# First layer batch by batch with rows sent in four groups, and units of 176 slots in place of 192 in the second FFN

## The chip, the cores and the metric

The kernel runs on one core of a Trainium2 chip. The metric is the device time in microseconds (us) of one execution. TensorE (PE in the rows, PEld for its weight loads), VectorE (DVE), ScalarE (ACT), GpSimd (POOL) and SyncE (SP) each work through their own instructions in order and wait for one another by semaphores.

## The reference, cut to what matters

```python
# x [4, 256, 256], ctx [4, 256, 64]; two layers, each mixes tokens and then runs an FFN
sim = einsum(Q, K) / ...; threshold = top_k(sim, 76)[..., -1:]        # per row of 256
A = sigmoid(sim) * (sim >= threshold); A = (A + A.T) * 0.5
x = x + tanh(g0) * ((1 - gamma) * layernorm(x) + gamma * A)           # layer 0, mixing
# layer 0, FFN: token n of a batch goes to expert n % 4 (gate/up 256 x 512, down 256 x 256)
x = x + tanh(g1) * (silu(gate) * up) @ down_proj[e]                   # on layernorm(x)
scores = (ctx Wq + bq)(ctx Wk + bk).T / 8 * layernorm(x)              # layer 1, mixing
x = x + tanh(g2) * softmax(where(mask, -inf, scores))
# layer 1, FFN: 64 experts of width 96, the best 8 per token, weights renormalised
x = x + tanh(g3) * sum_over_8(rw * (silu(h w_gate[e]) * (h w_up[e])) @ w_down[e])
```

The 1024 tokens make 8192 pairs of token and expert. Counted from the reference's own inputs, an expert gets 93 to 169 tokens.

## The kernel before

The tokens are eight tiles of 128 rows, two tiles per batch. The kernel has three stretches.

First stretch, all that leads to the rows of the second FFN. VectorE finds the 76th largest of each row of `sim` in ten rounds of eight (`keep_top`, L982: MAX8 and MATCH_REPLACE8 on `work`), adds the transposed adjacency (`mix_adjacencies`, L1012), takes the statistics of the layer norms (`statistics`, L962; GpSimd's `inverse_deviation`, L435, finishes them), adds the first FFN's result (`add_layer0`, L1023), does the masked scores and the softmax (`masked_scores`, L1030, `add_softmax`, L1045), and picks the experts (`choose_experts`, L1061) and the place of each row (`place_rows`, L1074). The order of its calls is written out at L1117 to L1154: the ten rounds of all four batches first, and the rest two batches at a time. The first FFN runs in two halves of two batches: eight steps of `expert_gate_up0` (L597) and `expert_down0` (L587) with 128 tokens each (`TE`, L48), whose product silu times up is GpSimd's (L443). TensorE, ScalarE and GpSimd follow orders written out by hand at L630 to L695, L873 to L919 and L452 to L492. The eight PSUM banks are handed round in the order of the list of fills (L221 to L277); each fill says whose count frees its bank, and all of ScalarE's share one count.

GpSimd sends the rows: `place_rows` on GpSimd (L469) issues 16 indirect DMAs per batch (L478), each of 128 rows of 320 floats, into `expert_rows` in HBM, which has room for 1024 rows per expert. Before the first of them it waits for `rows_cleared` (L475): SyncE's DMA at L349 has by then filled the first `CAP` rows of each of the 64 experts with empty rows, from `empty_rows`, of which `SLOTS` partitions hold `SUBS` rows each.

```python
sp.dma_start(by_expert[:, 0:CAP * ROW].rearrange("e (p n) -> p e n", p=SLOTS),
             empty_rows[0:SLOTS].rearrange("p (a i) d -> p a (i d)", a=1).to_broadcast([SLOTS, NE, SUBS * ROW])).then_inc(rows_cleared, 16)
```

Second stretch, the second FFN, once all 64 sends have landed (L369): 63 fixed units, one per expert 1 to 63, of `CAP` = 192 slots in two halves of `SLOTS` = 96. For each, SyncE loads the rows (L361, ten units ahead) and the weights (L355, L356, eight ahead), TensorE transposes the rows (L704), multiplies with gate and up (L715) and with down (L724), VectorE copies and multiplies (L1203, L1208), ScalarE takes silu and copies the result (L927, L933), and GpSimd scatters it with two indirect DMAs (L499) of 96 rows. Expert 0, and whatever of an expert lies beyond `CAP`, is done in a loop of counted length (L738); it runs once here.

Third stretch: the picks of each token are loaded and summed with its eight weights on TensorE (L770), and stored.

Of the kernel before, what the change touches and what calls it, by code (L numbers as in the profile page):

```python
# [11 lines left out]
ALU = mybir.AluOpType  # L12
ACT = mybir.ActivationFunctionType

P = 128
# [9 lines left out]
SLOTS = 96  # L25
# [9 lines left out]
def gated_layers_kernel(nc, x, ctx_in, mask_ss, mask_bs, g_xattn, g_ffn, wq0, wk0, gamma_raw, gate_up, down,  # L35
# [12 lines left out]
    TE = HALF // NE0  # L48
# [17 lines left out]
    with ExitStack() as stack:  # L66
# [118 lines left out]
        evac = {who: sem(who + "_evac") for who in ("act", "dve")}  # L185
# [35 lines left out]
        F_CTX, F_PROJ, F_SIM, F_SCORE = {}, {}, {}, {}  # L221
        F_CTX[0] = add_fill("ctx", "act")
# [9 lines left out]
        for b in range(B):  # L232
            F_SCORE[b] = add_fill("score", "act")


        F_ADJT, F_XNT, F_YT, F_XNT2, F_LOGIT = {}, {}, {}, {}, {}
        F_GATE, F_UP, F_DOWN = {}, {}, {}

        def add_gate_up_fills(q):
            F_GATE[q], F_UP[q] = add_fill("gate", "act"), add_fill("up", "act")  # L240

        def add_down_fill(q):
            F_DOWN[q] = add_fill("down", "act")

        for fill, name, who in ((F_ADJT, "adjt", "dve"), (F_XNT, "xnt", "act")):
            for b in (0, 1):
                fill[b] = add_fill(name, who)
        for q in range(NE0):
            if q == NE0 - 1:
                F_ADJT[2] = add_fill("adjt", "dve")  # L250
            add_gate_up_fills(q)
            if q:
                add_down_fill(q - 1)
        add_down_fill(NE0 - 1)
        F_XNT[2] = add_fill("xnt", "act")
        F_ADJT[3] = add_fill("adjt", "dve")
        F_YT[0], F_YT[1] = add_fill("yt", "dve"), add_fill("yt", "dve")
        F_XNT[3] = add_fill("xnt", "act")
        add_gate_up_fills(NE0)
        for q in range(NE0 + 1, 2 * NE0 - 1):  # L260
            add_gate_up_fills(q)
            add_down_fill(q - 1)
        F_XNT2[0], F_XNT2[1] = add_fill("xnt2", "act"), add_fill("xnt2", "act")
        add_gate_up_fills(2 * NE0 - 1)
        F_LOGIT[0], F_LOGIT[1] = add_fill("logit", "act"), add_fill("logit", "act")
        add_down_fill(2 * NE0 - 2)
        add_down_fill(2 * NE0 - 1)
        F_RANK = {}
        F_RANK[0], F_RANK[1] = add_fill("rank", "dve"), add_fill("rank", "dve")
        F_YT[2], F_YT[3] = add_fill("yt", "dve"), add_fill("yt", "dve")  # L270
        F_XNT2[2], F_LOGIT[2] = add_fill("xnt2", "act"), add_fill("logit", "act")
        F_XNT2[3] = add_fill("xnt2", "act")
        F_RANK[2] = add_fill("rank", "dve")
        F_LOGIT[3] = add_fill("logit", "act")
        F_RANK[3] = add_fill("rank", "dve")
# [13 lines left out]
        LAYERNORMS = ((0, None), (1, 0), (1, 1), (1, 2), (1, 3), (2, 0), (2, 1), (3, 0), (3, 1), (2, 2), (2, 3), (3, 2), (3, 3))  # L289
# [11 lines left out]
        def xn_t_view(k, b, permuted):  # L301

            if permuted:
                return xn_t[:, k].rearrange("p (f e b g) -> p f e b g", f=2, e=NE0, b=B // 2)[:, b // 2, :, b % 2, :]
            return xn_t[:, k, b * S:(b + 1) * S]
# [99 lines left out]
        def _(pool):  # L405
# [37 lines left out]
            def up_times_silu(half, experts):  # L443
                for e in experts:
                    q = half * NE0 + e
                    emptied(pool, F_UP[q])
                    if q >= 2:
                        pool.wait_ge(bank_filled, F_DOWN[q - 2] + 1)
                    pool.tensor_tensor(h0_t[:, q % 2].rearrange("p i t -> p (i t)"), silu0[:, q % 2], up0[:, q % 2],  # L449
                                       ALU.mult).then_inc(h0_ready, 1)  # L450
# [7 lines left out]
            inverse_deviation(1, 0)  # L458
            inverse_deviation(1, 1)
            up_times_silu(0, range(NE0))  # L460
            for n, b in ((1, 2), (1, 3), (2, 0), (2, 1)):
                inverse_deviation(n, b)
            up_times_silu(1, (0,))
            inverse_deviation(3, 0)
            up_times_silu(1, (1,))
            inverse_deviation(3, 1)
            up_times_silu(1, (2, 3))
# [14 lines left out]
            place_rows(0, 0, 2)  # L482
            inverse_deviation(2, 2)
            place_rows(0, 2, 4)
            inverse_deviation(2, 3)
            place_rows(0, 4, 10)
            inverse_deviation(3, 2)
            place_rows(0, 10, 13)
            inverse_deviation(3, 3)
            place_rows(0, 13, PICKS)  # L490
            for b in range(1, B):
                place_rows(b, 0, PICKS)  # L492
# [21 lines left out]
        def _(pe):  # L514
# [49 lines left out]
            for b in range(B):  # L564
                query_times_key(1, F_SCORE, b)

# [20 lines left out]
            def expert_down0(q):  # L587
                i = F_DOWN[q]
                begin(i)
                pe.wait_ge(h0_ready, q + 1)  # L590
                for hc in range(KC):
                    for ic in range(IC):
                        last = pe.matmul(bank(i)[:, hc * TE:(hc + 1) * TE], down_w[:, q % NE0, ic, hc * P:(hc + 1) * P],
                                         h0_t[:, q % 2, ic, :], start=ic == 0, stop=ic == IC - 1)
                last.then_inc(bank_filled, 1)
# [681 lines left out]
```

## Time and profile before

| | |
|---|---|
| median of 3 runs | 417.0 us (415.72 to 417.07) |
| the profiled execution | 417.87 us, of which its span is 416.1 us |
| first stretch, up to the last send's issue | 0 to 201.8 us |
| second stretch, first to last fixed scatter | 214.9 to 371.1 us |
| third stretch, first to last product | 383.0 to 413.5 us |
| busy: PE, DVE, ACT, POOL | 275.1, 210.7, 118.0, 214.0 us |

The times of stretches are read from the start and the duration of the instructions at their ends. A busy engine is not the bound by itself: what ended last is told by the chain of waits and by who stood idle.

### The profile page before, as it was taken

Reading aid. Unit: us, or ns where it says so; the run is one execution under the profiler, and the core shown is the slowest. Engines: PE = TensorE matmul, PEld = TensorE weight load, DVE = VectorE, ACT = ScalarE, POOL = GpSimd, SP = SyncE. Lnnn points to the kernel's source line nnn. Section 1 sums busy time; section 2 is a strip of 40 time slices with the busy share of each in tenths; the row PEclk is TensorE's granted clock in tenths of the full one; section 3 lists DMA queues with packets and bytes.
Section 4 is the critical chain, followed back from the end, with each engine's and each line's share of the span. In section 5 each row is a group of like instructions: output and inputs, shape, how many; then the busy total and the mean of one; then the engine's idle time right before and its main releaser. Section 6 shows DMA issues by size and latency. Waiting matters only on the chain.

```text
span 416.1 us, 5526 instructions
## 1 busy us (share of the span) xinstructions
PE 275.1 (66%) x1546; PEld 230.9 (55%) x1546; DVE 210.7 (51%) x921; ACT 118.0 (28%) x265; POOL 214.0 (51%) x256
## 2 busy tenths in 40 slices
PE   5898177137801610000199999999999999951997
PEld 1335067037800500000189999889999889931886
DVE  0799999989386679000033433343433343340352
ACT  2264353316634500000023333333333333320000
POOL 2622112013267777777327777777777777771000
PEclk9999999557975555555589999999999999995899
DMA  4899995360013333333498888888888887226891
GB/s 132 312 352 306 318 310 192 91 190 2 1 63 113 126 126 127 126 127 138 148 243 267 273 270 277 271 264 274 261 273 269 269 270 229 74 73 234 325 305 64
DMA packets 47374, 84.12 MB, mean 202 GB/s; under 512 B 10453, under 2 KB 28249, under 8 KB 46320
## 3 DMA queue, kind: packets, MB, share of 16 engines
q1 hardware_dynamic: 38128, 64.87, 49.9%
q0 software_dynamic: 9216, 18.90, 13.0%
q8 instruction: 13, 0.21, 0.2%
q14 instruction: 17, 0.14, 0.1%
HBM read 48.07 MB, written 39.85 MB: 211 GB/s over the span
## 4 chain that ended last, share of the span: by engine, by line
PE 52%; DVE 18%; POOL 16%; issue 7%; DMA 4%; ACT 2%; SPq 1%; POOLq 1%; ACTq 0%
PE psum L715 20%; POOL expert_rows L478 14%; PE psum L724 13%; PE psum L770 7%; PE psum L704 5%; DVE work L995 5%; DVE top L991 5%; DVE stats L966 2%; PE psum L536 2%; PE psum L530 2%; DMA sim<-token_picks 1%; POOL token_picks L499 1%; PE psum L604 1%; DVE adj L1000 1%; DMA gu_w<-expert_rows 1%
## 5 line engine op out<-in xcount | busy, mean ns | idle before, releaser
L499 POOL DMA_INDIRECT token_picks<-down_w,target x126 | 117.3, 931 | 54.9 <-issue 41.1
L715 PE MATMUL psum<-gu_w,wgu 128*96 128x192 f32 x504 | 93.7, 329 | 0.0
L715 PEld LDWEIGHTS psum<-gu_w,wgu 128*96 128x96 f32 x504 | 78.0, 165 | 0.6 <-DVE gu_w L1203 0.2
L478 POOL DMA_INDIRECT expert_rows<-x_rows,place_at x64 | 62.4, 975 | 23.8 <-issue 23.8
L724 PE MATMUL psum<-proj_t,gu_w 96*96 96x256 f32 x252 | 64.8, 379 | 0.0
L927 ACT ACTIVATE gu_w<-psum 96x192 f32<-96x192 f32 x63 | 20.6, 326 | 130.0 <-PE psum L715 130.0
L1208 DVE TENSOR_TENSOR gu_w<-gu_w,psum 96x192 f32<-96x192 f32 x63 | 22.1, 350 | 67.1 <-ACT gu_w L927 67.1
L704 PE MATMUL psum<-ident,gu_w 96*128 96x96 f32 x108 | 14.1, 256 | 53.1 <-DMA gu_w<-expert_rows 53.1
L933 ACT COPY down_w<-psum 96x512 f32<-96x512 f32 x63 | 36.6, 581 | 33.9 <-PE psum L724 33.9
L724 PEld LDWEIGHTS psum<-proj_t,gu_w 96*96 96x96 f32 x252 | 41.1, 163 | 7.1 <-DVE gu_w L1208 0.4
L704 PEld LDWEIGHTS psum<-ident,gu_w 96*128 96x128 f32 x108 | 12.5, 148 | 57.6 <-DMA gu_w<-expert_rows 54.4
L1203 DVE COPY gu_w<-psum 128x384 f32<-128x384 f32 x63 | 34.4, 547 | 0.0
L439 POOL TENSOR_TENSOR rstd<-var_eps,minus_half 128x2 f32<-128x2 f32 (+1 forms) x13 | 10.4, 797 | 46.6 <-DVE var_eps L972 46.5
L1202 DVE COPY target<-gu_w 96x2 uint32<-96x2 uint32 x27 | 4.5, 165 | 52.6 <-PE psum L704 52.6
L991 DVE MAX8 top<-work 128x8 f32<-128x256 f32 x72 | 26.8, 413 | 0.0
L995 DVE MATCH_REPLACE8 work<-top,work 128x256 f32<-128x256 f32 x64 | 25.7, 409 | 0.0
L604 PE MATMUL psum<-xn_t,gu_w 128*128 128x128 f32 x128 | 19.0, 316 | 1.7 <-ACT xn_t L832 1.7
L604 PEld LDWEIGHTS psum<-xn_t,gu_w 128*128 128x128 f32 x128 | 18.4, 231 | 2.4 <-issue 1.3
L449 POOL TENSOR_TENSOR h_t<-silu,up 128x256 f32<-128x256 f32 x8 | 6.1, 762 | 23.9 <-ACT up L849 23.6
L770 PE MATMUL psum<-sim,xn_t 128*128 128x256 f32 x32 | 9.9, 480 | 11.0 <-DMA sim<-token_picks 11.0
L1241 DVE TENSOR_TENSOR xs<-psum,scores 128x256 f32<-128x256 f32 x8 | 3.4, 424 | 27.3 <-PE psum L770 27.3
L583 PE MATMUL psum<-ident,x_rows 128*128 128x128 f32 x16 | 3.4, 351 | 20.8 <-ACT x_rows L827 19.8
(177 smaller groups left out, 397.1 us busy)
## 6 DMA issues: line engine op xcount, KB each, us to landing
expert_rows<-empty_rows SPq DMA_DIRECT2D x1, 15360.0 KB, 69.3
wgu<-in_L_ffn_w_gate_up SPq DMA_DIRECT2D x65, 192.0 KB, 2.9
gu_w<-expert_rows SPq DMA_DIRECT2D x28, 240.0 KB, 4.2
proj_t<-in_L_ffn_w_down SPq DMA_DIRECT2D x65, 96.0 KB, 4.0
sim<-expert_rows SPq DMA_DIRECT2D x18, 240.0 KB, 4.3
work<-expert_rows SPq DMA_DIRECT2D x18, 240.0 KB, 4.2
gu_w<-in_L_ffn_gate_up_proj SPq DMA_DIRECT2D x4, 512.0 KB, 8.2
sim<-token_picks SPq DMA_DIRECT2D x2, 1024.0 KB, 4.9
```

Source lines behind the costliest of these rows:

```text
L478: pool.indirect_dma_start(rows_dram, bass.IndirectOffsetOnAxis(ap=place_at[:, t, k:k + 1], axis=0), x_rows[:, t, :], None).then_inc(placed ...
L499: pool.indirect_dma_start(picks_dram, bass.IndirectOffsetOnAxis(ap=target[0:SLOTS, e % T_RING, i:i + 1], axis=0), y_slots[0:SLOTS, n, i, : ...
L604: last = pe.matmul(bank(fill)[:, ic * TE:(ic + 1) * TE], gu_w[:, e, k, c:c + P], xn_t[:, k, half * HALF + e * TE:half * HALF + (e + 1) * T ...
L704: last = pe.transpose(psum[:, e % 2, k * CAP + i * SLOTS:k * CAP + (i + 1) * SLOTS], x_slots[n][0:SLOTS, i, k * P:(k + 1) * P], ident[0:SL ...
L715: last = pe.matmul(psum[0:I1, 2 + e % 2, part * CAP:(part + 1) * CAP], wgu[:, n, k, part * I1:(part + 1) * I1], x_slots_t[:, e % 2, k, :], ...
L724: last = pe.matmul(psum[0:SLOTS, 4 + e % 2, i * D:(i + 1) * D], h1_t[:, e % 2, i * SLOTS:(i + 1) * SLOTS], wd[:, n, :], start=True, stop=True)
L770: last = pe.matmul(psum[:, t, 0:D], diag[:, t % 2, k, :], picks[t % K_RING][:, k * D:(k + 1) * D], start=k == 0, stop=k == TOP_K_EXPERTS - 1)
L933: act.copy(y_slots[0:SLOTS, n].rearrange("p i d -> p (i d)"), psum[0:SLOTS, 4 + e % 2, 0:SUBS * D]).then_inc(y_ready, 1)
L991: dve.max(top8[:, t, r], (work if r else sim)[:, t]).then_inc(top8_ready, 1)
L995: dve.match_replace(work[:, t], top8[:, t, r], (work if r else sim)[:, t], REMOVED).then_inc(rest_ready, 1)
L1203: dve.tensor_copy(x_slots_t[:, e % 2].rearrange("p k n -> p (k n)"), psum[:, e % 2, 0:KC * CAP]).then_inc(xt_copied, 1)
L1208: dve.tensor_tensor(h1_t[:, e % 2], silu1[:, e % 2], psum[0:I1, 2 + e % 2, CAP:2 * CAP], ALU.mult).then_inc(h_ready, 1)
```

## The change

`SLOTS` goes from 96 to 88 and so `CAP` from 192 to 176; the constant that divides a count by `CAP` goes from 683 to 745. `TE` goes from 128 to 64: the first FFN runs batch by batch in sixteen steps of 64 tokens. The orders of TensorE, ScalarE, VectorE and GpSimd are written anew, so that batch 0 goes through the whole first stretch while the later batches are still in their rounds; `keep_top` can be run for some of its rounds. Each kind of fill gets a count of its own. For steps 8 to 15 VectorE multiplies silu and up straight from PSUM in place of ScalarE's copy and GpSimd's product. GpSimd's sends are cut by the `inverse_deviation` calls of the later batches.

```diff
-SLOTS = 96
+SLOTS = 88
-    TE = HALF // NE0
+    TE = S // NE0
@@ fills
+        add_fills(("adjt", 0), ("score", 0), ("score", 1), ("xnt", 0), ("score", 2),
+                  ("gu", 0), ("gu", 1), ("gu", 2), ("adjt", 1), ("gu", 3), ("down", 0),
...
@@ gpsimd
             inverse_deviation(1, 0)
+            up_times_silu(0, 1, 2, 3)
             inverse_deviation(1, 1)
+            inverse_deviation(2, 0)
+            up_times_silu(4, 5, 6, 7)
             inverse_deviation(3, 0)
+            inverse_deviation(1, 2)
             place_rows(0, 0, 2)
+            inverse_deviation(2, 1)
+            place_rows(0, 2, 9)
+            inverse_deviation(3, 1)
+            place_rows(0, 9, PICKS)
+            place_rows(1, 0, 3)
+            inverse_deviation(1, 3)
+            place_rows(1, 3, 5)
             inverse_deviation(2, 2)
+            place_rows(1, 5, 10)
+            inverse_deviation(3, 2)
+            place_rows(1, 10, PICKS)
+            place_rows(2, 0, 3)
             inverse_deviation(2, 3)
+            place_rows(2, 3, 9)
             inverse_deviation(3, 3)
+            place_rows(2, 9, PICKS)
+            place_rows(3, 0, PICKS)
@@ tensor, one step of the first FFN
-            for part, fill in enumerate((F_GATE[q], F_UP[q])):
-                begin(fill)
+            begin(F_GU[q])
+            for part in range(2):
                     for ic in range(IC):
                         for k in range(KC):
-                            last = pe.matmul(bank(fill)[:, ic * TE:(ic + 1) * TE], gu_w[:, e, k, c:c + P],
+                            last = pe.matmul(bank(F_GU[q])[:, at:at + TE], gu_w[:, e, k, c:c + P],
@@ tensor, order (batch 0 and the end)
+            transpose_normed(F_XNT, xn, xn_ready, 0)
...
+            expert_gate_up0(0)
+            expert_gate_up0(1)
+            expert_down0(0)
...
+            expert_down0(15)
+            transpose_y0(3)
+            transpose_normed(F_XNT2, x_rows, x_rows_ready, 3)
             router_logits(3)
             rank_rows(3)
@@ vector, steps 8 to 15
+            def up_times_silu(*which):
+                for q in which:
+                    dve.wait_ge(silu0_ready, q - 2 * NE0 + 1)
+                    dve.wait_ge(down_step, q - 1)
+                    dve.tensor_tensor(h0_t[:, q % 2]..., silu0[:, q % 2], bank(F_GU[q])[:, IC * TE:2 * IC * TE], ALU.mult).then_inc(h0_ready, 1)
@@ vector, order
+            keep_top(1, 0, 2)
+            mix_adjacencies(0)
+            statistics(1, 0)
+            keep_top(1, 2, ROUNDS)
+            keep_top(2, 0, 1)
+            mix_adjacencies(1)
+            statistics(1, 1)
+            keep_top(2, 1, 4)
+            add_layer0(0)
+            statistics(2, 0)
+            keep_top(2, 4, 5)
+            masked_scores(0)
+            keep_top(2, 5, 7)
+            softmax_and_statistics(0)
+            keep_top(2, 7, ROUNDS)
+            choose_experts(0)
+            mix_adjacencies(2)
+            statistics(1, 2)
+            place_rows(0)
+            add_layer0(1)
+            statistics(2, 1)
+            keep_top(3, 0, 1)
+            masked_scores(1)
+            up_times_silu(8)
...
+            place_rows(1)
+            keep_top(3, 7, ROUNDS)
+            add_layer0(2)
+            mix_adjacencies(3)
+            statistics(1, 3)
+            statistics(2, 2)
+            masked_scores(2)
...
+            choose_experts(2)
+            up_times_silu(15)
+            place_rows(2)
+            add_layer0(3)
+            statistics(2, 3)
+            masked_scores(3)
+            softmax_and_statistics(3)
             choose_experts(3)
             place_rows(3)
```

## Rows read from the trace of the kernel before

**Rows 1.** The page: the chain that ended last, by engine, as shares of the span.

```profile
PE 52%; DVE 18%; POOL 16%; issue 7%; DMA 4%; ACT 2%; SPq 1%; POOLq 1%; ACTq 0%
```

**Rows 2.** Timeline of POOL, the sends: start, duration, instruction, idle before it.

```profile
116.09 1.23 POOL L478 DMA_INDIRECT expert_rows<-x_rows,place_at  x1 [5.18 <-issue]
...
131.40 0.73 POOL L439 TENSOR_TENSOR rstd<-var_eps,minus_half 128x2 f32<-128x2 f32 x1
...
132.57 1.04 POOL L478 DMA_INDIRECT expert_rows<-x_rows,place_at  x1 [0.16 <-issue]
...
199.60 0.96 POOL L478 DMA_INDIRECT expert_rows<-x_rows,place_at  x1 [0.30 <-issue]
200.86 0.96 POOL L478 DMA_INDIRECT expert_rows<-x_rows,place_at  x1 [0.30 <-issue]
```

**Rows 3.** DMA issues: size, and us from issue to landing.

```profile
expert_rows<-empty_rows SPq DMA_DIRECT2D x1, 15360.0 KB, 69.3
```

**Rows 4.** Timeline of SP, the issue of that DMA and the next.

```profile
16.19 0.61 SPq L349 DMA_DIRECT2D expert_rows<-empty_rows  x1
40.49 35.63 SPq L355 DMA_DIRECT2D wgu<-in_L_ffn_w_gate_up  x1
```

**Rows 5.** Windows: length; busy PE, PEld, DVE, ACT, POOL; granted clock, DMA share, GB/s.

```profile
50.00:60.00 10.00, 4.95 (x21) 4.24 (x22) 9.86 (x41) 5.02 (x10) 2.16 (x4) 1.00 1.00 333
60.00:66.00 6.00, 6.00 (x53) 6.00 (x52) 6.00 (x26) 2.51 (x7) 1.62 (x3) 1.00 0.70 234
...
72.00:74.00 2.00, 0.47 (x5) 0.28 (x3) 2.00 (x9) 1.48 (x3) 0.26 (x2) 1.00 0.18 49
...
116.00:130.00 14.00, 0.00 (x0) 0.00 (x0) 12.46 (x55) 4.45 (x14) 10.99 (x13) 0.60 0.26 94
```

**Rows 6.** Timeline of DVE: where its blocks begin.

```profile
32.81 0.75 DVE L991 MAX8 top<-sim 128x8 f32<-128x256 f32 x2
...
47.35 0.68 DVE L1016 TENSOR_TENSOR adj<-adj,psum 128x512 f32<-128x512 f32 x1
...
50.07 0.68 DVE L1016 TENSOR_TENSOR adj<-adj,psum 128x512 f32<-128x512 f32 x1
```

**Rows 7.** Windows, columns as in Rows 5: two batches' work on DVE after their rounds.

```profile
110.87:117.00 6.13, 3.92 (x40) 3.48 (x38) 5.71 (x34) 3.85 (x10) 0.95 (x2) 1.00 0.00 0
117.00:132.40 15.40, 0.00 (x0) 0.00 (x0) 13.72 (x59) 4.15 (x12) 12.07 (x16) 0.55 0.29 107
```

**Rows 8.** Timeline of PE: passes with 128 and with 64 columns.

```profile
94.06 5.80 PE L604 MATMUL psum<-xn_t,gu_w 128*128 128x128 f32 x32 [0.74 <-ACT xn_t L832]
...
107.75 1.95 PE L604 MATMUL psum<-xn_t,gu_w 128*128 128x128 f32 x16
109.53 1.90 PE L626 MATMUL psum<-router,xn_t 128*128 128x64 f32 x16
```

**Rows 9.** The chain in order of time: start, us, what, second FFN and end.

```profile
253.79 1.30 PE psum L715 x8
255.10 0.86 PE psum L724 x4
255.96 0.33 PE psum L704 x4
...
383.03 30.50 PE psum L770 x128
```

**Rows 10.** Timeline of POOL, the scatters.

```profile
214.94 0.94 POOL L499 DMA_INDIRECT token_picks<-down_w,target  x1 [13.13 <-ACT down_w L933]
...
355.29 0.91 POOL L499 DMA_INDIRECT token_picks<-down_w,target  x1 [0.78 <-issue]
356.50 0.91 POOL L499 DMA_INDIRECT token_picks<-down_w,target  x1 [0.30 <-issue]
...
371.14 2.88 POOL L499 DMA_INDIRECT token_picks<-down_w,target  x1 [0.30 <-issue]
```

**Rows 11.** Windows of the second FFN, columns as in Rows 5.

```profile
240.00:260.00 20.00, 20.00 (x130) 18.12 (x129) 7.79 (x24) 7.26 (x16) 14.66 (x17) 1.00 0.88 274
```

More of the change, by code:

```diff
@@ L231, in gated_layers_kernel @@
                 F_PROJ[w, half] = add_fill("proj", "act")
[L232 to L262, printed above, removed]
@@ L441, in inverse_deviation @@
                 pool.tensor_tensor(shift[:, n, tiles], neg_mean[:, n, tiles], rstd[:, n, tiles], ALU.mult).then_inc(shift_ready, 1)
[L443 to L448, printed above, removed]
+            def up_times_silu(*which):
+                for q in which:
+                    emptied(pool, F_GU[q])
+                    need(pool, down_step, q - 1)
                     pool.tensor_tensor(h0_t[:, q % 2].rearrange("p i t -> p (i t)"), silu0[:, q % 2], up0[:, q % 2],
@@ new lines, in _ @@
+            expert_down0(4)
+            expert_gate_up0(6)
+            expert_down0(5)
+            expert_gate_up0(7)
+            expert_down0(6)
+            expert_down0(7)
+            pe.wait_ge(consts_ready, 9)
+            transpose_normed(F_XNT2, x_rows, x_rows_ready, 0)
+            pe.wait_ge(ld["router"], 16)
+            router_logits(0)
+            transpose_y0(1)
+            transpose_adj(2)
+            rank_rows(0)
+            transpose_normed(F_XNT, xn, xn_ready, 2)
+            emptied(pe, F_XNT[2])
@@ L980, in _, with keep_top @@
                               ALU.mult).then_inc(evac["dve"], 1)
-            def keep_top(b):
+            def keep_top(b, first, end):
                 emptied(dve, F_SIM[b])
                 tiles = range(b * HB, (b + 1) * HB)
-                for r in range(ROUNDS):
+                for r in range(first, end):
                     for t in tiles:
@@ L1125, in _ @@
+            up_times_silu(8)
+            keep_top(3, 1, 2)
+            up_times_silu(9)
+            softmax_and_statistics(1)
+            keep_top(3, 2, 3)
+            up_times_silu(10)
+            keep_top(3, 3, 4)
+            up_times_silu(11)
+            keep_top(3, 4, 6)
+            choose_experts(1)
+            keep_top(3, 6, 7)
+            place_rows(1)
+            keep_top(3, 7, ROUNDS)
+            add_layer0(2)
             mix_adjacencies(3)
             statistics(1, 3)
-            for b in (0, 1):
-                add_layer0(b)
-                statistics(2, b)
@@ L1146, in _ @@
-            for b in (2, 3):
-                add_softmax(b)
-                statistics(3, b)
-            choose_experts(2)
-            router_weights(0)
-            place_rows(2)
+            statistics(2, 2)
+            masked_scores(2)
+            softmax_and_statistics(2)
+            up_times_silu(12, 13)
+            router_weights(0)
+            router_weights(1)
+            up_times_silu(14)
+            choose_experts(2)
+            up_times_silu(15)
+            place_rows(2)
```

324 lines of the change are left out of this document (166 added, 158 removed).

## The prediction, made before the changed kernel was run

> **What bounds the kernel now.** I read the chain of waits first: it is more than half TensorE, and the rest mostly VectorE and GpSimd [rows 1]. Then the timelines in order of time, since the shares mix three stretches. The reader is to see three different bounds.
>
> In the first stretch VectorE works nearly without a gap until 117 us, and from there GpSimd's sends set the end. They begin at 116.1 and the last ends at 201.8 [rows 2]. One costs 1.26 us from start to start (199.60 to 200.86), and each of the four `inverse_deviation` calls among them 1.17 us (131.40 to 132.57). 64 sends are 81 us and the four calls 5: GpSimd never rests, so the only way to end them earlier is to begin them earlier. In the second stretch TensorE is busy all of 20 us in a window of 20 [rows 11], and one unit is 1.30 + 0.86 + 0.33 = 2.49 us [rows 9]. But GpSimd is right behind: late in the stretch, where it is not waiting, its scatters start 1.21 us apart (355.29 to 356.50), 2.43 per unit [rows 10]. The third stretch (product of 30.5 us, rows 9) isn't touched.
>
> **The change, part by part.** All is counted in the profiled execution, 417.9 us; the median of the runs is 0.9 us below it.
>
> *When can the first send go?* VectorE must do, before batch 0 has its places: the start to 32.8, ten rounds each for batches 1 and 2 (14.5 us each with their last step, 32.81 to 47.35), three mixes with statistics (2.7 us each, 47.35 to 50.07) [rows 6], and batch 0's own rest. Rows 7 give that rest: 13.7 us busy for two batches from adding the FFN's result to the last statistics, 6.9 each; 5.7 for two batches from choice to places, 2.9 each. 32.8 + 29.1 + 8.2 + 6.9 + 2.9 = 79.9. To it come VectorE's waits. Most of TensorE's work for batch 0 (transposes, sixteen passes of gate and up, eight of down for each of four experts) lies beside rounds of batches 1 and 2, but the router's transposes and products stand directly ahead of the choice; I count 5 us for these waits, an estimate: eight of the router's passes at 0.12 [rows 8], a transpose, two copies, and two chains of the same kind (adjacency, FFN result) of which rounds cover only a part. So VectorE's side is ready at about 85, not 115.
>
> *What else must be there?* GpSimd waits for the empty rows ahead of its first send. Before, that wait was free: the DMA is issued at 16.19 [rows 4] and lands 69.3 us later [rows 3], at 85.5, with 30 us to spare. Now there is no slack left, and its shape changes with `SLOTS`: 88 partitions instead of 96. In bytes it is 8% less. How 88 partitions are dealt to 16 DMA engines no row of before shows, since all its transfers have 64, 96 or 128 partitions, all multiples of 16. The bounds: dealt evenly, 69.3 x 88/96 = 63.5 us, landing at 79.7. Dealt in equal parts of whole partitions, only 11 engines can share (8 each), each moving 8 partitions where it moved 6: 69.3 x 8/6 = 92.4 us, landing at 108.6. The windows say that engines differ: busy to the full until 60 us, 70% from 60 to 66, 18% (three of 16) from 72 to 74 [rows 5], and the next SP issue stays stuck from 40.5 to 76.1 behind the full queue [rows 4]. So the average engine ends at about 67 and the slowest near 85. Average times 8/6 from about 20 us, when the loads ahead of it are done: 83; slowest: 107. I take equal parts, and between 88 and 108 the middle, 98: the time depends on whether the slow engines are among the eleven, which no row tells.
>
> The Trainium skill ("DMA: Bandwidth & Descriptors", section "Why a DMA increments its semaphore by 16 and not by 1") speaks against this change: a DMA from SyncE runs on the largest number of engines up to 16 that divides the partition counts of both sides, so 96 gives 16 and 88 gives 11. With the slowest engine among the eleven, the sum would be that of the late rival below; with an even deal that of the early one. No row of before can confirm it.
>
> *From the first send to the last.* GpSimd's own floor is 64 sends and six calls, 64 x 1.265 + 6 x 1.17 = 88 us. The calls are now between the sends, and each waits for VectorE, which in turn goes on only once the call is done: a wait in both directions that was not there. Behind a waiting `inverse_deviation` stand the sends of its own engine. After the first send VectorE still has: ten rounds of batch 3 (14.5), three times 6.9 + 2.9, one mix (2.7), four steps of `up_times_silu` ahead of that and four behind (0.35 each, an estimate, 2.8), the weights of two batches (an estimate, 2): 51 us of work, and it needs TensorE's chain for each batch in turn. Walking the two orders against each other, GpSimd waits 1 us for the places of batch 1, 4 for the statistics of batch 3's mix, 3 to 7 for the places of batch 2, and little for those of batch 3. I take 12: 88 + 12 = 100 us, bounds 90 (nearly all covered) and 105. So the last send ends at 98 + 100 = 198, against 201.8: 3.8 us earlier.
>
> *TensorE in the first stretch.* Twice the steps with half the columns, and half the columns don't make a pass shorter: 16 passes with 128 columns took 1.95 us, 16 with 64 columns 1.90 [rows 8]. So the first FFN's 192 passes (128 in L604, 64 in L593) become 384, 192 x 0.12 = 23 us more. It is hidden where TensorE waited for VectorE's rounds; without that cover it costs all 23, and at the low clock 0.18 per pass (5.80 for 32, rows 8). The granted clock is 1.00 until 66 and 0.55 to 0.60 from 116 to 132 [rows 5, 7], so mostly the lower of the two levels (1.2 GHz in place of 2.4), after TensorE had stood idle. I count that as part of the 12 above.
>
> *ScalarE, PSUM, counts.* Four more table loads and one order more; ScalarE is 4.2 us busy in 15.4 [rows 7] and hides them. The separate counts cost nothing.
>
> *The second FFN.* TensorE: L715 moves 176 columns for 192, L704 88 for 96, L724's 256 stay: 1.30 x 11/12 + 0.33 x 11/12 + 0.86 = 2.35, 0.14 less per unit and 8.8 us in 63. But the scatters don't follow: they are 126 as before. A send of 128 rows has a pitch of 1.265 and a scatter of 96 one of 1.215; by that slope, 0.0016 per row, one of 88 has 1.20. So GpSimd is late next, and the stretch of scatters goes from 371.14 - 214.94 = 156.2 [rows 10] to 125 x 1.205 + 1.5 (the trace has three pauses of 0.5 like that before 355.29) = 152.1: 4.1 us less. The bounds: 1.265, if 88 partitions cost as 128 do, is 159.6, 3.4 us more; 8.8 us less, if GpSimd followed TensorE. The row loads: if on 11 engines, each of these carries 8/6 of its part. The share is 0.88 over all [rows 11], rows being 240 KB of some 670 KB per unit (274 GB/s x 2.5 us); 0.88 x (1 + 0.36 x 0.33) = 0.98. Just short of full, and ten units of lead cover a small lack, so I count nothing, and up to 5 us in the slow case. The loop for expert 0 still runs once: no expert has over 169 tokens, so 176 slots hold each.
>
> The sum: 417.9 - 3.8 - 4.1 = 410.0 us.
>
> **The rivals.**
>
> Early: the empty rows are dealt evenly and land by 80 to 85. Then VectorE sets the first send, at 85, and the last ends at 85 + 100 = 185, the scatters as above: 417.9 - 16.8 - 4.1 = 397.0. For it: the bytes get fewer. Against: 5.5 partitions per engine isn't a whole number.
>
> Late, and slower than before: the DMA with the slowest engines among the eleven lands at 108.6. The sends then end at 208.6, 6.8 us later than before, and batch by batch gains nothing, since the wait for VectorE has become a wait for the clearing. With the scatters 417.9 + 6.8 - 4.1 = 420.6, and up to 425 if the row loads on the same engines slow the units. It decides from a landing at 106 on (106 + 100 - 201.8 = 4.2, what the scatters give). For it: the tail of slow engines [rows 5]. Against: only eleven of sixteen are used, and fewer write at once.
>
> The first stretch is bound by TensorE: the 23 us of passes and the low clock lie on the chain of each batch (transpose, gate and up, down, transpose, logits), and the last send comes 7 us later than forecast, at 205: 417. For it: 0.60 of the clock in the thin part; against: idle TensorE in the same windows.
>
> **How the numbers follow.** Forecast case 0.40, early 0.30, TensorE 0.10, late 0.20. The likeliest is 410. The range goes from 394 (most of the early case) to 422. It leaves out 0.1 on either side. A measurement of this kernel can tell about 0.3%, 1.3 us. Faster: forecast and early, 0.70; same: the TensorE case, 0.10; slower: late, 0.20.
>
> **What would show it.** The landing of `expert_rows<-empty_rows`: by 85, near 98, or past 105; GpSimd's first send right behind it or behind `place_at`. The share of DMA while it runs: about 0.69 (11 of 16) if eleven engines. The last send 98 to 100 us after the first, with 12 us of GpSimd's idle time released by VectorE. In the second FFN TensorE has gaps (2.35 busy of 2.42), and the scatters stand 1.20 apart in every unit. A pitch of 1.26, or units released by DMA, would make the second half wrong; a first send at 85 the first.

## The result and the profile after

The changed kernel takes 456.7 us (median of 4 runs, 455.53 to 459.03) against 416.7 us before (415.72 to 417.07): the ratio is 1.097, with a 95% interval of 1.092 to 1.102. It is 9.7% slower, outside the range of the prediction. The span of the profiled execution is 455.4 us, against 416.1.

The chain that ended last in the changed kernel, as shares of the span (its answer before is [rows 1]):

```profile
PE 34%; POOL 18%; DMA 14%; issue 14%; DVE 9%; another core or an unknown queue 5%; ACT 3%; SPq 1%; POOLq 0%; DVEq 0%; ACTq 0%; PEldq 0%
```

TensorE and VectorE both have less of it; DMA went from 4% to 14% and unexplained waits ("issue") from 7% to 14%. Two of these names mislead. The 5% of "another core or an unknown queue" is the wait for the clearing, 21.6 us from 102.5 on. And of DMA's 14% the page puts 11 on the scatters of the second FFN, whose landing frees the buffers that ScalarE copies into; but GpSimd rests there only its 0.30 us between two scatters, so it is GpSimd that sets the pace, and ScalarE waits behind it. What was lost, and where, is told by the timeline of GpSimd (start, duration, instruction, idle before it and what ended it), which answers to [rows 2, 10]:

```profile
101.47 0.78 POOL L414 TENSOR_TENSOR rstd<-var_eps,minus_half 128x2 f32<-128x2 f32 x1 [12.13 <-DVE var_eps L993]
...
124.41 1.24 POOL L448 DMA_INDIRECT expert_rows<-x_rows,place_at  x1 [21.88 <-DMA expert_rows<-empty_rows]
...
153.83 0.95 POOL L448 DMA_INDIRECT expert_rows<-x_rows,place_at  x1 [7.22 <-issue]
...
161.76 0.72 POOL L414 TENSOR_TENSOR rstd<-var_eps,minus_half 128x2 f32<-128x2 f32 x1 [4.45 <-DVE var_eps L993]
...
190.49 0.96 POOL L448 DMA_INDIRECT expert_rows<-x_rows,place_at  x1 [9.25 <-issue]
...
233.52 0.96 POOL L448 DMA_INDIRECT expert_rows<-x_rows,place_at  x1 [0.31 <-issue]
...
248.87 1.02 POOL L476 DMA_INDIRECT token_picks<-down_w,target  x1 [14.38 <-ACT down_w L954]
...
300.86 0.99 POOL L476 DMA_INDIRECT token_picks<-down_w,target  x1 [0.30 <-issue]
302.16 0.99 POOL L476 DMA_INDIRECT token_picks<-down_w,target  x1 [0.30 <-ACT down_w L954]
...
410.89 1.06 POOL L476 DMA_INDIRECT token_picks<-down_w,target  x1 [0.30 <-issue]
```

The reader is to see four things: the first send comes 8.3 us later than before, not earlier, and GpSimd stood 21.88 us ahead of it until the clearing had landed; it was held up even before that, at 101.5, by VectorE's statistics; there are three long pauses among the sends; and a scatter takes 0.99 us, with 1.30 from start to start. The whole loss can be laid out on these rows:

| piece, us | before | after | difference |
|---|---|---|---|
| start to first send | 116.09 | 124.41 | +8.3 |
| first to last send | 84.77 | 109.11 | +24.3 |
| last send to first scatter | 14.08 | 15.35 | +1.3 |
| first to last fixed scatter | 156.20 | 162.02 | +5.8 |
| from there to the end of the span | 44.96 | 44.51 | -0.5 |
| span | 416.1 | 455.4 | +39.3 |

The windows of the changed kernel, columns as in [rows 5]:

```profile
50.00:60.00 10.00, 10.00 (x50) 10.00 (x49) 2.88 (x9) 0.87 (x4) 0.91 (x2) 1.00 0.68 177
...
78.00:84.00 6.00, 6.00 (x30) 6.00 (x30) 3.43 (x14) 3.93 (x8) 0.63 (x2) 1.00 0.48 102
...
84.00:90.00 6.00, 6.00 (x30) 6.00 (x30) 3.80 (x15) 1.42 (x4) 1.31 (x3) 1.00 0.48 99
...
114.00:120.00 6.00, 0.00 (x0) 0.00 (x0) 0.00 (x0) 0.33 (x1) 0.00 (x0) 1.00 0.58 124
```

In 50 to 60 TensorE is busy throughout and VectorE less than a third, where before VectorE was busy 9.86 of 10 and TensorE half. The DMA share is 0.68, which is 11 of 16, where it was 1.00, and from the early seventies 0.48. From 114 to 120 all four engines stand still but for 0.33 us of ScalarE.

TensorE's timeline has the first FFN's passes, in blocks of 16 and 32, and the router's, answering to [rows 8]:

```profile
43.77 7.09 PE L584 MATMUL psum<-xn_t,gu_w 128*128 128x64 f32 x32
...
58.33 3.52 PE L584 MATMUL psum<-xn_t,gu_w 128*128 128x64 f32 x16
...
94.89 1.94 PE L606 MATMUL psum<-router,xn_t 128*128 128x64 f32 x8 [0.78 <-issue]
```

Sixteen passes of 64 columns take 3.52 us, 0.22 each; in [rows 8] sixteen of them took 1.90, and sixteen of 128 columns 1.95. The router's eight take 0.24 each. The granted clock in these windows is 1.00.

### The profile page after: what moved, and what is told of

The parts are those of the page before. It is cut to its first block, busy times and chain, and to the rows that moved or that the text cites. A ratio compares the mean times of both kernels' runs of the same rounds, so it can differ in the third digit from the quotient of the medians.

```text
span 455.4 us, 5963 instructions
## 1 busy us (share of the span) xinstructions
PE 335.5 (74%) x1738; PEld 282.0 (62%) x1738; DVE 207.3 (46%) x929; ACT 117.7 (26%) x269; POOL 219.1 (48%) x256
## 3 DMA queue, kind: packets, MB, share of 16 engines
q0 software_dynamic: 9216, 18.92, 12.5%
## 4 chain that ended last, share of the span: by engine, by line
PE 34%; POOL 18%; DMA 14%; issue 14%; DVE 9%; another core or an unknown queue 5%; ACT 3%; SPq 1%; POOLq 0%; DVEq 0%; ACTq 0%; PEldq 0%
DMA token_picks<-down_w,target 11%; PE psum L584 9%; POOL token_picks L476 9%; POOL expert_rows L448 7%; PE psum L774 7%; PE psum L570 6%; PE psum L719 3%; DVE top L1011 2%; DVE work L1015 2%; PE psum L728 2%; POOL rstd L414 2%; PE psum L557 1%; PE psum L513 1%; DVE stats L987 1%
## 5 line engine op out<-in xcount | busy, mean ns | idle before, releaser
L719 PE MATMUL psum<-gu_w,wgu 128*96 128x176 f32 x504 | 88.1, 319 | 0.0
L728 PE MATMUL psum<-proj_t,gu_w 96*88 96x256 f32 x252 | 66.3, 385 | 3.7 <-DVE gu_w L1262 3.2
L1262 DVE TENSOR_TENSOR gu_w<-gu_w,psum 96x176 f32<-96x176 f32 x63 | 21.0, 333 | 95.5 <-ACT gu_w L948 90.8
L954 ACT COPY down_w<-psum 88x512 f32<-88x512 f32 x63 | 36.7, 582 | 92.9 <-DMA token_picks<-down_w,target 79.6
L584 PE MATMUL psum<-xn_t,gu_w 128*128 128x64 f32 x256 | 57.1, 421 | 2.2 <-ACT xn_t L831 2.2
L584 PEld LDWEIGHTS psum<-xn_t,gu_w 128*128 128x128 f32 x256 | 55.9, 332 | 4.1 <-ACT xn_t L831 3.4
L728 PEld LDWEIGHTS psum<-proj_t,gu_w 96*88 96x88 f32 x252 | 37.0, 156 | 17.5 <-DVE gu_w L1262 9.5
L570 PE MATMUL psum<-h_t,down_w 128*128 128x64 f32 x128 | 30.1, 422 | 17.4 <-DVE h_t L1056 17.4
L570 PEld LDWEIGHTS psum<-h_t,down_w 128*128 128x128 f32 x128 | 28.8, 332 | 17.6 <-issue 17.6
L1257 DVE COPY gu_w<-psum 128x352 f32<-128x352 f32 x63 | 32.3, 513 | 0.0
L1011 DVE MAX8 top<-work 128x8 f32<-128x256 f32 x72 | 26.8, 413 | 0.6 <-DVE h_t L1056 0.6
```

Source lines behind the costliest of these rows:

```text
L570: last = pe.matmul(bank(i)[:, c:c + TE], down_w[:, e, ic, hc * P:(hc + 1) * P], h0_t[:, q % 2, ic, :], start=ic == 0, stop=ic == IC - 1)
L584: last = pe.matmul(bank(F_GU[q])[:, at:at + TE], gu_w[:, e, k, c:c + P], xn_t[:, k, b * S + e * TE:b * S + (e + 1) * TE], start=k == 0, st ...
L719: last = pe.matmul(psum[0:I1, 2 + e % 2, part * CAP:(part + 1) * CAP], wgu[:, n, k, part * I1:(part + 1) * I1], x_slots_t[:, e % 2, k, :], ...
L728: last = pe.matmul(psum[0:SLOTS, 4 + e % 2, i * D:(i + 1) * D], h1_t[:, e % 2, i * SLOTS:(i + 1) * SLOTS], wd[:, n, :], start=True, stop=True)
L954: act.copy(y_slots[0:SLOTS, n].rearrange("p i d -> p (i d)"), psum[0:SLOTS, 4 + e % 2, 0:SUBS * D]).then_inc(y_ready, 1)
L1011: dve.max(top8[:, t, r], (work if r else sim)[:, t]).then_inc(top8_ready, 1)
```

## The experiments

The theory after the result had three causes. P: with only 64-column passes TensorE is so slow that each batch's chain waits for it. C: the clearing of 88 partitions lands at 124. S: a scatter of 88 rows costs more than one of 96. The rivals: the batch-by-batch order itself (two-way waits between GpSimd and VectorE); one cause that makes the others; row loads on 11 engines. Ratios are to the kernel before, in runs on the same chip.

**The new orders alone.**

```diff
# on the changed kernel
-SLOTS = 88
+SLOTS = 96
-    dve.tensor_scalar(n_over_i[:, 0], n_over[:], 745.0, None, ALU.mult)
+    dve.tensor_scalar(n_over_i[:, 0], n_over[:], 683.0, None, ALU.mult)
```

> The new orders and steps alone, with 192 slots as before. If the clearing on eleven engines is what is late (landing at 124 in the changed kernel), it lands at 85.5 again, VectorE's places of batch 0 (102.5 us) release the first send, and the last send ends 109 us after the first, at about 212; scatters take 156 us as before, and the time is about 427 us, slower than before by 2 to 3%. If instead the wait for the clearing hides something that is late anyway, first send and last send move less, and the time stays above 435. If the new orders are good and 176 slots alone cost, the last send ends before 202 and the time is below 417.

432.2 us, ratio 1.037 (1.034 to 1.040). The first and the last send:

```profile
104.49 1.23 POOL L448 DMA_INDIRECT expert_rows<-x_rows,place_at  x1 [1.75 <-issue]
...
216.06 0.96 POOL L448 DMA_INDIRECT expert_rows<-x_rows,place_at  x1 [0.30 <-issue]
```

No wait for the clearing; it landed 68.4 us after its issue. Yet the send is at 104.5, not at 85, and 111.6 us pass to the last, 2.6 more than was expected; the time is 5 us above the 427 expected. So the new orders with their 64-column passes lose without the 88 slots too; the first send's gain of 11.6 us is less than the 26.8 that the sends take longer.

**176 slots alone.**

```diff
# on the kernel before
-SLOTS = 96
+SLOTS = 88
-    dve.tensor_scalar(n_over_i[:, 0], n_over[:], 683.0, None, ALU.mult)
+    dve.tensor_scalar(n_over_i[:, 0], n_over[:], 745.0, None, ALU.mult)
```

> The kernel before with 176 slots in place of 192, orders untouched. If 88 partitions cost what the changed kernel shows, the scatters start 1.295 us apart and take 162 us (5.8 more), the DMA share while clearing is 0.68, and the clearing lands at 105 to 124, where the first send was at 116, so the last send moves by 0 to 8: 424 to 432 us. If the dearer scatter belongs to the new orders, the stretch takes 152 and the time is 413 to 417.

432.7 us, ratio 1.038 (1.035 to 1.041). First send, a window, and two scatters:

```profile
125.84 1.24 POOL L478 DMA_INDIRECT expert_rows<-x_rows,place_at  x1 [14.58 <-DMA expert_rows<-empty_rows]
...
386.00 0.99 POOL L499 DMA_INDIRECT token_picks<-down_w,target  x1 [0.30 <-issue]
387.30 0.99 POOL L499 DMA_INDIRECT token_picks<-down_w,target  x1 [0.30 <-issue]
```

```profile
50.00:60.00 10.00, 5.07 (x21) 4.35 (x22) 9.86 (x40) 5.02 (x10) 2.16 (x4) 1.00 0.68 178
```

Even in the old order, which had 30 us to spare, the clearing holds the first send, by 9.8 us against 116.1; and the scatters start 1.30 apart and take 161.8 us. These are the two prices that were expected, and the time is just past the upper end of the 424 to 432. The late landing belongs to the 88 partitions and to nothing in the new orders.

**Clear from 96 partitions, the rest as changed.**

```diff
# on the changed kernel
-sp.dma_start(by_expert[:, 0:CAP * ROW].rearrange("e (p n) -> p e n", p=SLOTS), empty_rows[0:SLOTS]...
+sp.dma_start(by_expert[:, 0:96 * SUBS * ROW].rearrange("e (p n) -> p e n", p=96), empty_rows[0:96]...
```

> The changed kernel with its empty rows still written from 96 partitions (192 rows per expert, as before), all else at 88. If the number of partitions decides on how many engines a DMA runs, the DMA share is near 1.00 while clearing, the landing is near 85, the first send goes at 103 in place of 124, and with the same 109 us from first to last send the time is about 435 us (21 less than the changed kernel). If the clearing was slow because TensorE, VectorE and ScalarE now work beside it, it lands past 105 still, and the time is above 445.

438.6 us, ratio 1.052 (1.049 to 1.055), with the first send at 104.3 as expected and the last at 215.9, like those with 96 throughout; the 109 us between them that the expected 435 took from the changed kernel are 111.6. So the landing of the clearing costs 18.1 us of the 456.7. The scatters' stretch is 161.8 us, as in the changed kernel; what that costs is told by the last run of this part, which computes the same and differs from this one only in having row loads and scatters on 96 partitions. One window of this run says something of the passes:

```profile
108.00:114.00 6.00, 6.00 (x30) 6.00 (x30) 4.12 (x19) 1.46 (x3) 4.73 (x5) 0.50 0.32 113
```

TensorE makes 30 passes in 6 us at a granted clock of 0.50, and 30 in 6 us at 1.00 (the changed kernel's window 78 to 84). The 64-column passes run at the same rate at both readings. The kernel before has passes of 128 columns at about that rate where the reading is 0.50: 18 of its L604 begin between 94.1 and 98, 0.22 us each.

**Twice the columns in the same passes.** Each pass of the first FFN moves its 64 columns twice (the second copy goes into columns that the next pass overwrites): twice the work, the same number of passes.

```diff
# on the changed kernel (in the down product likewise, but for the last pass of a bank)
-last = pe.matmul(bank(F_GU[q])[:, at:at + TE], gu_w[:, e, k, c:c + P],
-                 xn_t[:, k, b * S + e * TE:b * S + (e + 1) * TE], start=k == 0, stop=k == KC - 1)
+last = pe.matmul(bank(F_GU[q])[:, at:at + 2 * TE].rearrange("p (r t) -> p r t", r=2), gu_w[:, e, k, c:c + P],
+                 xn_t[...].rearrange("p (r t) -> p r t", r=1).to_broadcast([P, 2, TE]), start=k == 0, stop=k == KC - 1)
```

> The changed kernel with every pass of the first FFN moving its 64 columns twice (128 columns, the second copy is overwritten), so more work for TensorE in the same number of passes; results are the same. If the passes take 0.21 us because TensorE's clock is at its lower level when it streams so few columns, they go back to 0.11 to 0.12, the last send ends 10 or more us sooner and the time is about 445. If 0.21 us is what such a pass costs by itself (weights loaded for 64 columns), the passes get longer or stay, and the time is 456 or more.

446.7 us, ratio 1.072 (1.069 to 1.075): twice the work is 10 us faster. TensorE's timeline, then GpSimd's:

```profile
53.48 1.95 PE L585 MATMUL psum<-xn_t,gu_w 128*128 128x128 f32 x16
```

```profile
125.86 1.24 POOL L448 DMA_INDIRECT expert_rows<-x_rows,place_at  x1 [40.50 <-DMA expert_rows<-empty_rows]
...
223.40 0.96 POOL L448 DMA_INDIRECT expert_rows<-x_rows,place_at  x1 [0.30 <-issue]
```

Sixteen passes take 1.95 us in place of 3.52. GpSimd now waits from 85.4 on and not from 102.5, and VectorE has batch 0's places at 86.2 and not at 103.3; the sends take 97.5 us in place of 109.1. The wait for the clearing has swallowed the first 17 us; only the second gain shows.

**Both.** The last kernel with 96 slots again.

```diff
# on the kernel with twice the columns
-SLOTS = 88
+SLOTS = 96
-    dve.tensor_scalar(n_over_i[:, 0], n_over[:], 745.0, None, ALU.mult)
+    dve.tensor_scalar(n_over_i[:, 0], n_over[:], 683.0, None, ALU.mult)
```

> The changed kernel with 192 slots and with the doubled columns of e4. If clearing, scatters and the clock at which the passes run are the whole loss, the clearing lands at 84.5, VectorE sets the first send at about 86 (in e4 GpSimd stood ready from 85.4 us on), the last send ends 98 us later (e4) at about 184, 18 us sooner than in the kernel before, the scatters take 156, and the time is about 399 us: faster than the kernel before by 4%. If batch by batch holds another cost that the late clearing covered in e4, the last send ends after 190 and the time is above 405.

402.9 us, ratio 0.967 (0.964 to 0.970): 3.3% faster than the kernel before, 4 us above the expected 399, since 101.4 us pass between the sends in place of 98.

```profile
86.89 1.23 POOL L448 DMA_INDIRECT expert_rows<-x_rows,place_at  x1 [1.75 <-issue]
...
188.24 0.96 POOL L448 DMA_INDIRECT expert_rows<-x_rows,place_at  x1 [0.30 <-issue]
```

**The shorter unit without its price.** Computes 176 slots; the clearing, the row loads and the scatters use 96 partitions.

```diff
# on the kernel of "both"
+SLOTS = 88
+MOVED = 96
-pool.indirect_dma_start(..., target[0:SLOTS, ...], y_slots[0:SLOTS, n, i, :], ...)
+pool.indirect_dma_start(..., target[0:MOVED, ...], y_slots[0:MOVED, n, i, :], ...)
# and so in the clearing DMA, the row load and the copy of target
```

> Computes on 176 slots, but clears, loads and scatters 96 partitions, and doubles the columns as e4. If the dearer scatter comes from 88 partitions in the DMA and not from the shorter unit, the scatters start 1.215 to 1.22 us apart all through, the stretch of scatters takes 152 to 154 us where 192 slots take 156, TensorE has gaps, and the time is 2 to 4 us below e5. If TensorE's shorter unit counts in full, the stretch takes 148 and the time is 8 below e5. If the shorter unit itself makes the scatters dearer, they are 1.295 apart and the time is 6 us above e5.

401.3 us, ratio 0.963 (0.961 to 0.965), the fastest of all.

```profile
202.62 0.96 POOL L477 DMA_INDIRECT token_picks<-down_w,target  x1 [12.76 <-ACT down_w L957]
...
354.25 0.92 POOL L477 DMA_INDIRECT token_picks<-down_w,target  x1 [0.30 <-issue]
355.47 2.81 POOL L477 DMA_INDIRECT token_picks<-down_w,target  x1 [0.30 <-issue]
358.89 1.02 POOL L488 DMA_INDIRECT token_picks<-down_w,over_target  x1 [0.62 <-issue]
```

The stretch of scatters is 152.9 us against 156.2 with 192 slots: 3.4 less, though by the count of the prediction TensorE has 8.8 less to do. In the kernel before one unit took 2.50 us, which is TensorE's 2.49; here GpSimd's two scatters, 2 x 1.22, set the pace. The last of them took 2.81 us and the loop's, still of 88 rows, 1.0, which gives some back: the time is 1.6 us below that of "both", where 2 to 4 were expected, and the two intervals overlap. So the gain of the shorter unit is small and barely measured.

**Rows per scatter.** On the kernel before, thirteen units each (eleven for the last) scatter 96, 88, 90, 92 and 86 rows.

```diff
# on the kernel before
+rows = (96, 88, 90, 92, 86)[min(e // 13, 4)]
-pool.indirect_dma_start(..., target[0:SLOTS, ...], y_slots[0:SLOTS, n, i, :], ...)
+pool.indirect_dma_start(..., target[0:rows, ...], y_slots[0:rows, n, i, :], ...)
```

> The kernel before, whose scatters take 96 partitions in units 0 to 12, 88 in 13 to 25, 90 in 26 to 38, 92 in 39 to 51 and 86 in 52 to 62 (no slot beyond partition 84 holds a row, so results are the same). If the cost of a scatter goes with its rows, all lie within 0.01 us of 1.215. If it goes with the count being no multiple of 16, as the 0.99 us for 88 in place of 0.915 for 96 suggests, 88, 90, 92 and 86 are dearer than 96: alike if only the odd count matters, and dearer the fewer engines can share equally (90: 15, 88: 11, 92: 4, 86: 2) if the deal matters.

A single run: 436.8 us against 416.6. Rows out of each block, in that order:

```profile
231.83 0.92 POOL L500 DMA_INDIRECT token_picks<-down_w,target  x1 [0.30 <-issue]
...
265.06 0.99 POOL L500 DMA_INDIRECT token_picks<-down_w,target  x1 [0.30 <-ACT down_w L934]
266.35 0.99 POOL L500 DMA_INDIRECT token_picks<-down_w,target  x1 [0.30 <-issue]
...
298.00 0.93 POOL L500 DMA_INDIRECT token_picks<-down_w,target  x1 [0.30 <-issue]
299.24 0.94 POOL L500 DMA_INDIRECT token_picks<-down_w,target  x1 [0.30 <-issue]
...
333.40 1.17 POOL L500 DMA_INDIRECT token_picks<-down_w,target  x1 [0.30 <-issue]
334.88 1.18 POOL L500 DMA_INDIRECT token_picks<-down_w,target  x1 [0.30 <-issue]
...
368.21 1.42 POOL L500 DMA_INDIRECT token_picks<-down_w,target  x1 [0.30 <-issue]
369.94 1.43 POOL L500 DMA_INDIRECT token_picks<-down_w,target  x1 [0.30 <-issue]
```

96, 88, 90, 92 and 86 rows cost 0.92, 0.99, 0.94, 1.18 and 1.43 us of GpSimd. The cost doesn't follow the number of rows. It follows the largest divisor of the number up to 16, which is 16, 11, 15, 4 and 2. The Trainium skill ("DMA: Bandwidth & Descriptors", section "Why a DMA increments its semaphore by 16 and not by 1") has that divisor as the number of engines of a DMA, for those that GpSimd issues too, some direct copies aside; no row here shows the engines of a scatter, only this order of its costs.

**Clearing 104 partitions.**

```diff
# on the kernel before
-by_expert[:, 0:CAP * ROW].rearrange("e (p n) -> p e n", p=SLOTS), empty_rows[0:SLOTS]...
+by_expert[:, 0:104 * SUBS * ROW].rearrange("e (p n) -> p e n", p=104), empty_rows[0:104]...
```

> The kernel before with its empty rows written from 104 partitions (208 rows per expert, 8% more bytes). 104 has 13 as its largest divisor up to 16, 8 partitions per engine as 88 has on 11. If whole equal parts are dealt, the DMA share while clearing is 13/16 = 0.81, and the landing is as late as with 88, 108 to 126, seen as GpSimd's wait ahead of its first send. If the deal is even, the share is 1.00 and the landing is near 92, with no wait; then 88 was slow for another reason.

426.6 us in a single run; the windows and the first send:

```profile
50.00:60.00 10.00, 5.10 (x22) 4.38 (x23) 9.86 (x40) 5.02 (x10) 2.16 (x4) 1.00 0.80 202
84.00:90.00 6.00, 2.79 (x12) 2.42 (x12) 4.55 (x14) 0.00 (x0) 0.00 (x0) 0.52 0.61 125
```

```profile
125.92 1.23 POOL L478 DMA_INDIRECT expert_rows<-x_rows,place_at  x1 [14.71 <-DMA expert_rows<-empty_rows]
```

The share is 0.80 (13 of 16), the landing the same as with 88 partitions though there are 18% more bytes. It looked as if the time were set by the partitions per engine, eight in both cases. The next two runs say that this alone isn't the cause.

**Clearing 128 and 112 partitions.** The same edit with 128, and with 112.

> The kernel before with the clearing DMA on 128 partitions, 256 rows per expert in place of 192, nothing else changed: 16 engines with 8 partitions each, as many partitions per engine as with 88 or 104. If the slow engines fall to some 13 GB/s each because each has 8 partitions, the DMA share stays at 1.00 until 72 us, then falls to about 0.8, the rate then is some 170 GB/s (13 per engine), and the first send goes at about 125 as with 88 and 104. If the landing with 88 is late because fewer than 16 engines share it, 128 partitions land at about 16 + 69.3 x 8/6 = 108, and the first send goes at 116 as before.

> The kernel before with the clearing DMA on 112 partitions, 16 engines with 7 each; 128 partitions landed 57.4 us after issue, 96 after 69.3, although they write a third more. If only a full set of 128 partitions is fast, 112 lands at 69.3 x 7/6 = 80.9 us or later, with a share that falls in steps between 60 and 90 us. If the rate simply rises with the partitions, it lands in between, after 60 to 65 us, with the share at 1.00 to the end.

The DMA issues (size, us to landing) and a window of each, first of 128, then of 112:

```profile
expert_rows<-empty_rows SPq DMA_DIRECT2D x1, 20480.0 KB, 57.4
```

```profile
50.00:60.00 10.00, 5.02 (x21) 4.30 (x22) 9.86 (x41) 5.02 (x10) 2.16 (x4) 1.00 1.03 413
```

```profile
expert_rows<-empty_rows SPq DMA_DIRECT2D x1, 17920.0 KB, 61.3
```

```profile
50.00:60.00 10.00, 5.01 (x21) 4.30 (x22) 9.86 (x41) 5.02 (x10) 2.16 (x4) 1.00 1.01 359
```

128 partitions, eight per engine on all sixteen, land after 57.4 us, with a third more bytes than the 96 that took 69.3 [rows 3]. So neither landing that the first of these texts gives holds (125 or 108). Of the second the landing by a rising rate does, with 61.3 in between; the share at 1.00 to the end doesn't, for it is 0.82 from 66 to 72 and 0.70 from 72 to 74, ahead of the landing at about 78. The kernel with 112 took 415.1 us in a single run: the clearing's landing is hidden there, as in the kernel before.

**The shorter unit with the passes as changed.** As "the shorter unit", on the changed kernel with its 64-column passes.

> The changed kernel with its 64-column passes as they are, but with all that moves rows for the second FFN (the clearing DMA, the row loads, the scatters) on 96 partitions, and the computation on 176 slots. Theory (three separate causes): the clearing no longer holds the first send, which goes at 104.4 as in the two runs with 96 partitions cleared, and the last at 216; the scatters then take 152.9 us instead of 162.0, so 438.6 - 9.1 = 429.5 us, 3% slower than before, and the 28 us to the same kernel with wide passes (401.3) are the passes' alone. Rival (the shorter unit matters by itself once all is on 96): under 425. Rival (the gain of the scatters was the wide passes' in part): 433 or more.

> The same kernel as the run before with 64-column passes and all moves on 96 partitions: there the second FFN of every kernel, the one before too, ran some 60 us longer than in the other runs, by slower loads, so its stretch said nothing. Expected as then: first send at 104.4, last at 216 to 219, scatters 152.9 us, 429.5 us in all; rivals under 425 (the shorter unit matters by itself) and 433 or more (the scatters' gain was the wide passes' in part).

The first of the two ran on a chip where the kernel before took 481.8 us too (its time was 492.2), with some 60 us more from the last send to the last scatter, in its trace and in that of clearing 128 partitions, which shared that chip (477.2). Only its first stretch is used, with the first send at 104.3, and of clearing 128 only the landing. For landings the chip makes no difference that shows: 96 partitions took 68.1 us on it and 68.2 to 69.3 on the others. The second gave 430.2 us, ratio 1.031 (1.026 to 1.035), with the first send at 104.2 and the last at 215.8, 0.7 from the expected 429.5. "The new orders alone", 96 slots throughout, took 432.2: here too the shorter unit gains some 2 us, and here too the intervals overlap. From this kernel to the one of 401.3 us the passes' columns are the only difference: 28.9 us. From "clear from 96 partitions" to it, 438.6 to 430.2, the row loads and scatters are: 8.4 us, where the scatters' stretch shrinks by 9.1 (161.8 to 152.6). The row loads on eleven engines cost nothing that shows.

## Why the prediction was wrong

*VectorE ready for the first send at 85: the sum was right, a term ahead of it wrong.* In the changed kernel VectorE had the places at 103.3, with doubled columns at 86.2. There its waits between 32.8 and the places add up to 4.8 us (in "both"), so 79.9 of work and 5 of waits were well counted; in the changed kernel they add up to 22.4, the longest of them ahead of the choice of experts:

```profile
97.17 0.35 DVE L1099 MAX8 l_top<-logits 128x8 f32<-128x64 f32 x2 [9.33 <-ACT logits L860]
```

What failed is the step "half the columns don't make a pass shorter ... 192 x 0.12 = 23 us more. It is hidden". The row for 0.12 [rows 8] is of 64-column passes with 128-column passes right ahead of them. In a stretch that has only 64-column passes each takes 0.22. The groups of instructions by line show the size of it. Before, the first FFN's products took 19.0 + 8.5 = 27.5 us of TensorE for 192 passes:

```profile
L604 PE MATMUL psum<-xn_t,gu_w 128*128 128x128 f32 x128 | 19.0, 316 | 1.7 <-ACT xn_t L832 1.7
...
L593 PE MATMUL psum<-h_t,down_w 128*128 128x128 f32 x64 | 8.5, 278 | 2.4 <-POOL h_t L449 2.4
```

In the changed kernel:

```profile
L584 PE MATMUL psum<-xn_t,gu_w 128*128 128x64 f32 x256 | 57.1, 421 | 2.2 <-ACT xn_t L831 2.2
...
L570 PE MATMUL psum<-h_t,down_w 128*128 128x64 f32 x128 | 30.1, 422 | 17.4 <-DVE h_t L1056 17.4
```

That is 87.2 us, so 59.7 more and not 23. The cover that hid 23 doesn't hide 60: TensorE is full where VectorE waits (50 to 60 us above). The TensorE rival had the right mechanism with the wrong price, 7 us, and a chance of 0.10; the low clock that it added isn't in the readings, which are 1.00.

*The clearing lands at 98: right mechanism, wrong size.* Eleven engines were said, with a share of 0.69; it was 0.68. By the Trainium skill ("DMA: Bandwidth & Descriptors", section "Why a DMA increments its semaphore by 16 and not by 1"), 88 partitions go on eleven engines, and 104 would go on thirteen; the shares 0.68 and 0.80 agree. But the landing is at 124, beyond even the late bound of 108.6. The step that failed is "69.3 x 8/6": it takes an engine's rate as fixed. What follows on single engines is an estimate from the windows. Eleven engines move 177 GB/s until about 72 us; then three of them are done (the share drops by 3/16) and eight go on at 99 to 102 GB/s, 12.5 each. The three had 25 each. Eight at 12.5 GB/s need 105 us for their 1.31 MB each (14,080 KB / 11), which ends at 124 if they begin at about 19, when the loads ahead of them are done. With 104 partitions the same two rates come out: 125 GB/s from ten, 77 from three. With 112 and 128 partitions sixteen engines average 22 and 26 GB/s in the windows shown. Why eight of eleven get half the rate isn't settled: neither the number of engines (thirteen did no better) nor eight partitions per engine (128 did best) explains it alone. The late rival named the wait, in its place, and from where it decides, but gave it 420.6 and a chance of 0.20.

*100 us from the first to the last send: right for passes at full rate.* Counted like the forecast, to the end of the last send, it was 110.1 in the changed kernel, and 98.5, 102.3 and 102.9 with doubled columns. The floor of 88 plus the pauses of the rows above, 7.2 + 4.5 + 9.2, is 109. So with passes at full rate the two-way waits of the new order cost 10 to 15 us, where 12 were counted, and the slow passes add the rest. The rival that the new order itself is the loss falls: in "both" the same order gains 13.6 us.

*Second FFN 4.1 us shorter: wrong sign.* The scatters' stretch is 162.0 us, 5.8 longer. The step that failed is the slope, "0.0016 per row", drawn through 96 and 128 rows, two numbers that divide by 16; 88 doesn't, and costs 0.99 us, more than a send of 128 rows at 0.96 [rows 2]. The pitch of 1.295 is beyond the upper bound of 1.265. What the term stood on was right: GpSimd is next behind TensorE. With its moves on 96 partitions the stretch is 152.9, where 152.1 was forecast for a pitch of 1.205. The row loads were counted at nothing, and nothing of them shows: 125 scatters 0.075 us further apart make the 9.1 us.

*The sum.* Each of three terms was wrong against the change, and two of them are ahead of the same instruction. From 456.7 us, cured passes alone give 9.9, cured moves alone 26.4 (430.2), and both 55.3 (401.3): 19.0 us come only with the pair, since the first send waits for the later of the two. The early rival, 397.0, counts the change without late clearing and without dear passes; 401.3 and 402.9 are near it. The chance of 0.70 for faster was too high for one plain reason: none of the four cases took a 64-column pass above what rows of 128 columns show, 0.12 or 0.18, and all took a scatter at 1.205, so none of them covered an error in these rows.

## What to carry to other kernels

Halving the columns of a pass, or taking a few partitions off a transfer, isn't a smaller step of the same kind: look for rows of the same shape in the same company, and where there is none, bound the price by what a doubling would do. Before cutting a tile's partitions, see whether the new number still divides by 16; computing on 88 and moving 96 kept the shorter unit's gain, some 2 us, without the price. And where two waits end at one instruction, the cure of one shows little; try both before giving either up.

## What the runs showed of the hardware

- TensorE: sixteen passes with 128-column weights and 64 columns, float32, took 3.52 us in a stretch of their own, with 128 columns 1.95 us; the granted clock read 1.00 in both, and at a reading of 0.50 the short ones were no slower (30 in 6 us). At that reading passes of 128 columns take 0.22 us too in the kernel before. So the short ones went as long ones go at the lower level, whatever the reading; whether the clock is behind it, or the loads of the weights, no run here separates.
- A DMA from SyncE that clears 64 experts, by partitions: 88, 96, 104, 112, 128 landed about 108, 69, 109, 61 and 57 us after issue (for 88 and 104 the profile gives no landing; theirs is read from the send that waited for it). More bytes can be faster: 20,480 KB on 128 partitions landed 51 us earlier than 14,080 KB on 88.
- GpSimd's time for an indirect DMA: 0.92 us for 96 rows, 0.94 for 90, 0.99 for 88, 1.18 for 92 and 1.43 for 86.
